# LoRA A's product z in matmuls of 128 columns a tile, in place of 256 columns a group

## The reference

```python
x = x + _L0_ffn_ref(_L0_cond_ref(x, cond_128, ...), ...)
x = x + _L1_ffn_ref(_L1_cond_ref(x, cond_128, ...), ...)

# _L0_cond_ref: a 64 x 64 mix of the channels, made per batch entry from 8 experts
out = jnp.einsum('boi,bih->boh', agg_w, x) + agg_b[:, :, None]          # y

# _L0_ffn_ref: a dense product and two LoRA paths, one chosen by a gate per 256 rows, one shared
base_out = jnp.matmul(x, kernel) + bias
Ax = jnp.einsum('bri,bti->btr', A_eff, x_flat)                          # z, rank 32
delta_flat = jnp.einsum('bor,btr->bto', B_eff, Ax)
Ax_s = jnp.einsum('ri,bti->btr', lora_A_shared, x_flat)                 # z, rank 32, shared
delta_flat = delta_flat + jnp.einsum('or,btr->bto', lora_B_shared, Ax_s)
```

## Time and profile before

| | |
|---|---|
| median of 3 runs | 800.48 us (798.65 to 801.49) |
| profiled execution | 804.9 us |
| its span on the core | 803.1 us |
| TensorE busy | 779.6 us, 97% of the span |
| VectorE, ScalarE, GpSimd busy | 526.9, 208.9, 83.9 us |
| mean granted clock of TensorE | 0.989 of full speed |
| `z_group`, all 8 | 128 matmuls and 128 weight loads |

### The profile page before, as it was taken

How to read it: one execution, slowest core, us unless ns; L and a number is a source line. 1 busy time by engine, 2 the same in 40 slices (tenths; PEclk the granted TensorE clock), 3 DMA queues, 4 the chain that set the end, 5 groups by cost and what they waited for, 6 DMA issues and landing times.

```text
span 803.1 us, 10383 instructions
## 1 busy us (share of the span) xinstructions
PE 779.6 (97%) x3881; PEld 656.0 (82%) x3881; DVE 526.9 (66%) x636; ACT 208.9 (26%) x254; POOL 83.9 (10%) x56
## 2 busy tenths in 40 slices
PE   7988799999999999989999999999999999999998
PEld 5757688888888899868888888888888888888886
DVE  4656695436344379987777769877754796655552
ACT  5431010100000030433333337333333742111110
POOL 3141452231322100000000000000000000000000
PEclk9999999999999999989999999999999999999999
DMA  8967763464575799345444214278773664444441
GB/s 231 213 202 225 194 183 94 124 151 110 139 157 134 175 244 246 108 111 143 139 137 131 79 69 178 78 219 242 223 242 111 226 244 158 158 166 174 157 169 66
DMA packets 87275, 131.45 MB, mean 164 GB/s; under 512 B 11080, under 2 KB 64824, under 8 KB 84552
## 3 DMA queue, kind: packets, MB, share of 16 engines
q1 hardware_dynamic: 84064, 129.93, 56.1%
q10 hardware_dynamic: 3064, 0.90, 0.6%
q0 software_dynamic: 112, 0.17, 0.1%
HBM read 78.20 MB, written 51.72 MB: 162 GB/s over the span
## 4 chain that ended last, share of the span: by engine, by line
PE 81%; DMA 9%; DVE 6%; SPq 3%; issue 1%; ACT 1%; POOL 0%; DVEq 0%
PE ps L1827 37%; PE ps L1589 25%; PE ps L1887 19%; DMA raw<-in_L_ffn_lora_B_shared 2%; DMA raw<-in_L_ffn_kernel 2%; DVE cr L1293 2%; DMA lora_b_scratch<-lb_c_lo 1%; DMA a_scratch<-w_a_f 1%; DVE cf L1299 1%; DVE cf L1285 1%; SPq L358 1%; DMA lb<-lora_b_scratch 1%; SPq L438 1%; DMA c_scratch<-c_st 1%; DVE c_st L1299 1%
## 5 line engine op out<-in xcount | busy, mean ns | idle before, releaser
L1827 PE MATMUL ps<-cr,w_s_hi 128*128 128x512 f32 x512 | 159.8, 394 | 4.1 <-ACT s L919 4.1
L1827 PE MATMUL ps<-cr,w_a_hi 128*128 128x512 f32 x384 | 118.4, 389 | 0.0
L1827 PEld LDWEIGHTS ps<-cr,w_s_hi 128*128 128x128 f32 x512 | 97.3, 190 | 25.2 <-issue 4.9
L1827 PE MATMUL ps<-cr,w_s_lo 128*128 128x512 f32 x256 | 100.6, 393 | 0.0
L1827 PEld LDWEIGHTS ps<-cr,w_a_hi 128*128 128x128 f32 x384 | 72.0, 188 | 14.9
L1589 PE MATMUL ps<-wk_hi,y_hi 128*128 128x512 f32 x256 | 81.1, 398 | 2.0 <-DVE cb_c L1165 1.2
L1589 PE MATMUL ps<-wk_lo,y_hi 128*128 128x512 f32 x256 | 79.2, 391 | 0.0
L1589 PE MATMUL ps<-wk_hi,y_lo 128*128 128x512 f32 x256 | 78.8, 389 | 0.0
L743 POOL TENSOR_TENSOR x_t<-x_in,f_bias 128x1024 f32<-128x1024 f32 x16 | 63.5, 3973 | 137.5 <-DMA x_scratch<-x_t 137.5
L1146 DVE TENSOR_TENSOR x_t<-ps,x_t 128x1024 f32<-128x1024 f32 x16 | 19.5, 1223 | 86.7 <-PE ps L1589 86.7
L1827 PE MATMUL ps<-cr,w_a_lo 128*128 128x512 f32 x192 | 74.7, 389 | 0.0
(11 more groups left out here) (174 smaller groups left out, 1242.5 us busy)
## 6 DMA issues: line engine op xcount, KB each, us to landing
x_scratch<-x_t SPq DMA_DIRECT2D x128, 64.5 KB, 2.1
x<-x_scratch SPq DMA_DIRECT2D x32, 258.0 KB, 6.6
x_in<-in_x SPq DMA_DIRECT2D x16, 512.0 KB, 5.8
r_scratch<-r_t SPq DMA_DIRECT2D x16, 512.0 KB, 3.1
h_scratch<-s SPq DMA_DIRECT2D x32, 256.0 KB, 2.3
h_f<-h_scratch SPq DMA_DIRECT2D x8, 1024.0 KB, 5.9
res<-r_scratch SPq DMA_DIRECT2D x16, 512.0 KB, 5.0
raw<-in_L_ffn_w SPq DMA_DIRECT2D x56, 128.0 KB, 4.4
```

Source lines behind the costliest of these rows:

```text
L1827: last = pe.matmul(o, l, r, start=first and q == 0 and n == 0, stop=q == 3 and n == 2, skip_group_check=True)
```

## The change

`z_group` makes the two tiles of a group one after the other. The wait for `y_lo_made`, which stood once for the whole group, stands ahead of each tile and asks for that tile's split alone. Each product has 128 columns in place of 256, so there are 32 of them a group and not 16, each with its weight load. The other engines' programs are the same.

```diff
             def z_group(g, s, first=False):
 
                 pe.wait_ge(la_gathered, g + 1)
-                pe.wait_ge(y_lo_made, g * 4 + 4)
                 if not first:
                     pe.wait_ge(z_taken, g)
-                dst = bank(6)[:, 0:ROWS_G]
-                for k in range(KT):
-                    mm(dst, la_g[s][:, k, :], y_hi[s][:, :, k, :], k == 0, False)
-                    last = mm(dst, la_g[s][:, k, :], y_lo[s][:, :, k, :], False, k == KT - 1)
+                for a in range(TG):
+                    pe.wait_ge(y_lo_made, g * 4 + 2 * a + 2)
+                    dst = bank(6)[:, a * P:(a + 1) * P]
+                    for k in range(KT):
+                        mm(dst, la_g[s][:, k, :], y_hi[s][:, a, k, :], k == 0, False)
+                        last = mm(dst, la_g[s][:, k, :], y_lo[s][:, a, k, :], False, k == KT - 1)
                 last.then_inc(z_mm, 1)
```

## The result

| | before | after |
|---|---|---|
| median of the timed runs | 800.99 us (4 runs, 798.65 to 805.02) | 813.96 us (4 runs, 812.97 to 815.87) |
| profiled execution | 804.9 us | 813.05 us |
| its span | 803.1 us | 811.2 us |

The changed kernel is slower: the ratio is 1.0144, 95% interval 1.0096 to 1.0192, so +1.0% to +1.9%. (The ratio isn't that of the two medians, which would be 1.0162; it makes +11.5 us, the medians +13.0.) The forecast was 811.0 us, range 804.6 to 814.0, which holds the 813.96, by 0.04 us. A later set of runs beside the kernel before gave 811.54 against 801.85, ratio 1.0123 (1.0082 to 1.0164).

The account below looks back on a forecast made before the run. TensorE, 97% busy and never idle from 106 to 277 us, was taken to bound the kernel. Six groups +11.4, first two +0 and clock -0.9 made +10.5 us, 811.0 us against the median; range 804.6 to 814.0.

Parts of the forecast that it names:

- Place: TensorE from 106 to 277 us, six of eight z_group calls: never idle, so added time moves all that follows; +11.4 us.
- Price: Each 128-column product in z_group costs 0.119 us, low end 0.106; a group 3.81 us against 1.91, +1.90.
- The weight load as the cause: In z_group each product has its own weight load, and the next matmul follows that load by 0.12 us, whatever the columns.
- The first two groups, +0: z_group(0) and z_group(1) end u_tile(2) 2.9 us later, covered by TensorE's 4.1 us wait for lb; +0.
- It doesn't move: The DMA chain behind the 4.1 us wait for lb starts from lora_b work before z, so it stays put.
- The clock, -0.9: Shorter waits before slow stretches may keep TensorE's clock up; one of two pays at most, -1.7 us at even chance, half taken.
- The extra wait costs nothing: Added wait on y_lo_made mid-group costs nothing, as both tiles' splits are done before the group's u_lora ends.
- The range: 804.6 to 814.0 us: the forecast's bounds 807.7 to 813.4, reaching down to the partly hidden case, 804.6.
- Columns only: Rival in z_group: weight load hides, a product costs 0.066 us; six groups +1.2, 801.7 us, no change; chance 0.08.
- partly hidden: Rival in z_group: a product costs 0.086 us, a group +0.84, six +5.0; 804.6 us; chance 0.06.
- A gain from the earlier start: Rival: starting tile a's half before tile b's split pays only where z waits for y_lo, 0.4 us once; worth 0.
- Changed form: Rival in z_group: narrow products become two records each, a group 6.8 us, together +34; 833 us; chance 0.07.

Follow-up runs that it names:

- early_y5: Against the kernel before: y_tile(4), y_tile(5) and four k-tiles of u_tile(3) ahead of the lb wait, VectorE's take of tile 5's y earlier; 794.75 us, ratio 0.9913.
- half_w: Changed kernel with one wait a group and 64 of 128 weight columns loaded per product, half of z left out; 802.38 us, ratio 1.0009 to the kernel before.
- first2: Kernel before with 128-column products in z_group 0 and 1 alone, the other six at 256; 802.35 us, ratio 1.0005.
- last6: Kernel before with 128-column products in z_group 2 to 7 alone, the first two at 256; 809.89 us, ratio 1.0107.
- onewait: Changed kernel, all eight groups narrow, with one wait for both tiles' split; 812.93 us, ratio 1.012 to the kernel before, beside 811.54 for the changed kernel.
- late_lb: Kernel before, z at 256 columns, with y_tile(4) and four k-tiles of u_tile(3) moved ahead of the wait for group 1's LoRA B; 803.15 us, ratio 1.0024.

## Why the prediction was right, point by point

- **Place.** "In that stretch a longer `z_group` has nothing to hide behind": shown. The stretch is 181.2 us in all three profiled kernels with six narrow groups and no wait at `z_group(2)`, and 171.1 in those with wide ones, `early_y5` among them (95.23 to 266.35).
- **Price, mis-sized.** I took 0.119 us a product and kept 0.106 as the low end; it is 0.11 (32 in 3.52 us). The step that was off is "A load thus follows a matmul's start and the next matmul follows that load by 0.12, whatever the columns". That holds for 256 columns, where the loads wait for the matmuls. With 128 the loads run on by themselves, 0.11 us apart, and a matmul follows its load by 0.06; the distance that repeats is the one between the two loads in the earlier trace rows. A group costs 3.52 - 1.91 = +1.61 in itself and 0.05 more in the `mix` products behind it (108.40 to 110.15, 1.75 us in place of 1.70), +1.66; the stretch gives 10.06/6 = +1.68. I had +1.90. The six: +11.4 forecast, +10.1 measured. The low end of +8.9 was 1.2 too low, the forecast 1.3 too high.
- **The weight load as the cause.** Argued from the earlier trace rows before, shown by `half_w` now. The 81 ns a pair of the Trainium skill ("TensorE: Matmul & The Clock Gate", section "Back-to-back issue gap") don't hold for this type at 128 columns: 111 ns. The same page's section "LDWEIGHTS (loading the stationary operand)" gives P / 1.2 ns for P columns of weights, which makes 107 and 53 ns for 128 and 64, an estimate. The trace agrees, with 0.11 and 0.05 us from load to load after a wait.
- **The first two groups, +0.** The result is shown by `first2`, the way to it was off. I had 1.4 + 1.5 = 2.9 us arriving at the wait for `lb`. From the start of `z_group(0)` to the end of `u_tile(2)` the trace of after has 25.31 us in place of 24.92, +0.4. The wait on `y_f` took up 1.1 of it (2.08 to 0.97) and not 0.5, since one of VectorE's takes of z was 0.57 us shorter in this execution. The 0.43 on `y_lo` went as forecast, and the early slow stretch was gone (next point). The wait for `lb` is 2.9 us after and 2.8 in `first2`, a little outside the 1.2 to 2.7. "It doesn't move" isn't contradicted, but it is seen only within a wide scatter: counted from the start of `z_group(0)`, that wait ends after 29.0 us before and 26.7 in `last6`, and after 27.6 to 28.3 us in the three profiles with narrow first groups.
- **The clock, -0.9.** I said that one of the two slow stretches pays at most. The early one did: the 16 `mix` records behind the short wait at 65.39 take 2.2 us, 0.17 of them a wait, and not 3.16. What that saved went into the wait for `lb`. Behind that wait the clock fell all the same (16 records in 3.15 us, 87.14 to 90.29). To `z_group(2)` only 0.3 us came back, so the term should have been near 0.
- **The extra wait costs nothing.** Shown: 150.38 us with it and without it, in the comparison of `onewait`. But "both tiles' splits are done" was read from one execution, where the split of tile 5 ended at 106.0 and z began at 106.56: half a microsecond. In an execution without the wait for `lb` it isn't done, so the sentence was right by luck there.
- **Medians.** The medians of the two sets give +13.0 and +9.7 us (by the ratios +11.5 and +9.9), the traces +10.1 for the stretch. The scatter is in the set-up: `z_group(0)` begins at 59.52, 58.89, 61.09 (the changed kernel again), 55.51 and 56.27 us in five profiles and `z_group(2)` at 106.56, 104.88, 107.21, 100.00 and 101.67. Behind it the stretch to the convolution repeats to 0.01 us, and what follows takes 525.1 to 525.8 us in four of them and 523.5 in the fifth. I see no second mechanism, and none was shown.
- **The range.** My own bounds ended at 813.4; the 814.0 of the range has no working behind it. That 813.96 lies within is luck: the traces give +10.1 where the forecast had +10.5, and the 3 us between that and the first set's +13.0 are scatter as far as the traces tell.
- **Rivals.** Columns only (0.066 us) and partly hidden (0.086): excluded by the 0.11. A gain from the earlier start: `z_group(1)` did start before tile 3's split was done (69.54, the split ends at 70.29), and what it saved went into the waits behind it. Changed form: excluded, 256 records for 256 products.

## What to carry to other kernels

In these runs a product with its own weights costs the longer of two times, the streaming of its columns and the load of its weights; in float32r here the load of 128 columns takes 0.11 us, so cutting 256 moving columns to 128 nearly doubles the price of the work, and an earlier start has to win that back. Look for the wait that the earlier start would remove before cutting: here it was 0.4 to 0.8 us, once, in front of a longer one. And a wait on a DMA is a cover with a bottom: what is put in front of it was free here within what the runs can tell (`first2`), but taking the wait away (6.5 us in the end) needs the step behind it, here a split that was queued behind other work, to be early too.

## What was not expected of the hardware

- With 64 columns a product, TensorE's granted clock fell to 0.50 in every group while the engine was never idle in it: 0.11 us from start to start became 0.21, and 12.4 us more were lost in the products behind the six groups.
- Half the weights, 64 columns, make a narrow float32r product cost 0.06 us in place of 0.11. From load to load after a wait it is 0.05 us for 64 columns of weights and 0.11 for 128.
- VectorE's two `y_lo` of 128x512 took 1.29 us in one execution and 5.1 in another, with GpSimd's addition of 3.8 us beside them. Tile 4's split shows the same: 8.04 us before, with GpSimd's two additions (8.18 us) beside it, and 1.48 us in `late_lb`, where it comes before GpSimd starts (88.24). That this is a contention between the two is likely by these overlaps, but no run took GpSimd's work away to show it.
